# Expert rows of a mixture-of-experts layer in 24 blocks of two 64-row halves, each half with an expert of its own, instead of 31 blocks of 128 rows with one

## The reference

```python
logits = jnp.einsum('th,eh->te', x, gate_w)              # 1024 tokens, 16 experts
topk_w, topk_idx = jax.lax.top_k(softmax(logits), 2)
combine = jnp.sum(one_hot(topk_idx, 16) * topk_w[..., None], axis=1)
gu = jnp.einsum('th,ehj->etj', x, w_gate_up)             # 256 -> 2 x 176
h = silu(gu[..., :176]) * gu[..., 176:]
y = jnp.einsum('eti,eih,te->th', h, w_down, combine)     # 176 -> 256
y = y + swiglu(x @ shared_gate_up, 352) @ shared_down
```

## Time and profile before

| | us |
|---|---|
| runs | 254.44, 252.72, 254.32 |
| median | 254.32 |
| the profiled execution | 252.71 |
| its span (first to last instruction) | 250.7 |

### The profile page before, as it was taken

One profiled execution on the slowest core, in us unless ns is written; L12 is line 12 of the kernel. 1 busy time (PEld: TensorE's weight loads), 2 busy tenths in 40 slices (PEclk: granted clock), 3 DMA queues, 4 the chain that ended last, 5 costly groups with the idle time before them and its releaser, 6 DMA issues.

```text
span 250.7 us, 5232 instructions
## 1 busy us (share of the span) xinstructions
PE 237.4 (95%) x1660; PEld 177.2 (71%) x1660; DVE 148.5 (59%) x452; ACT 129.3 (52%) x465; POOL 92.5 (37%) x110
## 2 busy tenths in 40 slices
PE   8969799999999999999999999799999999999995
PEld 6635475666766677898788787567777777777784
DVE  1568888887889856437896588653223232323184
ACT  2146988989889898540524216124343434343440
POOL 2111211112111100102662004655777777777460
PEclk9999999999999999999999999999999999999999
DMA  7999877100005400006013000222333333343495
GB/s 217 267 366 387 283 174 171 53 3 3 3 0 160 171 3 3 1 3 229 1 41 129 0 3 4 63 68 81 105 105 107 105 95 112 89 102 111 144 338 188
DMA packets 20388, 28.10 MB, mean 112 GB/s; under 512 B 2369, under 2 KB 17355, under 8 KB 20363
## 3 DMA queue, kind: packets, MB, share of 16 engines
q1 hardware_dynamic: 16683, 19.01, 24.5%
q0 software_dynamic: 2976, 8.13, 11.0%
q10 hardware_dynamic: 704, 0.64, 0.8%
HBM read 21.61 MB, written 6.16 MB: 111 GB/s over the span
## 4 chain that ended last, share of the span: by engine, by line
PE 71%; ACT 13%; DVE 8%; issue 4%; DMA 1%; POOL 1%; ACTq 0%; POOLq 0%; DVEq 0%
PE bank L898 15%; PE bank L910 11%; ACT pr_s L1010 10%; PE bank L829 8%; PE bank L531 5%; PE bank L573 4%; PE bank L560 3%; PE bank L879 3%; PE bank L889 3%; PE bank L658 2%; PE bank L536 2%; PE bank L623 2%; PE bank L649 1%; PE bank L668 1%; DMA qx_s<-ffn_in,prT 1%
## 5 line engine op out<-in xcount | busy, mean ns | idle before, releaser
L1010 ACT ACTIVATE pr_s<-bank,mx 128x128 f32<-128x128 f32 x128 | 45.2, 383 | 8.0 <-DVE mx L1236 8.0
L898 PE MATMUL bank<-gu_s,bxT 128*128 x124 | 41.7, 460 | 0.2 <-DVE bxT L1561 0.2
L1567 DVE TENSOR_TENSOR pr_s<-bank,pr_s 128x176 f32<-128x176 f32 x31 | 10.6, 341 | 51.6 <-ACT pr_s L1165 50.9
L492 POOL DMA_INDIRECT expert_out<-by,prT x31 | 31.0, 1000 | 14.8 <-ACT by L1000 7.5
L487 POOL DMA_INDIRECT qx_s<-ffn_in,prT x31 | 30.1, 972 | 14.6 <-issue 8.2
L1000 ACT ACTIVATE prT<-bank 128x512 f32<-128x512 f32 (+1 forms) x63 | 31.1, 497 | 2.9 <-PE bank L573 1.8
L910 PE MATMUL bank<-dn_s,prT 88*128 x124 | 31.7, 379 | 0.0
L1010 ACT ACTIVATION_READ_ACCUMULATOR pr_s<-bank,mx 128x1 f32 x128 | 28.6, 224 | 0.0
L898 PEld LDWEIGHTS bank<-gu_s,bxT 128*128 128x128 f32 x124 | 21.2, 190 | 7.2 <-issue 0.4
L1000 ACT ACTIVATE by<-bank 128x256 f32<-128x256 f32 x31 | 11.9, 383 | 23.5 <-PE bank L910 21.9
L1236 DVE TENSOR_REDUCE mx<-bank 128x4 f32<-128x512 f32 x32 | 20.5, 683 | 4.7 <-PE bank L560 4.7
(11 more groups left out here) (194 smaller groups left out, 438.2 us busy)
## 6 DMA issues: line engine op xcount, KB each, us to landing
gu_s<-in_w_gu SPq DMA_DIRECT2D x8, 704.0 KB, 7.0
dn_s<-in_w_dn SPq DMA_DIRECT2D x4, 704.0 KB
gu_s<-in_ctx_in SPq DMA_DIRECT2D x2, 512.0 KB, 9.2
ffn_in<-x_s SPq DMA_DIRECT2D x4, 256.0 KB, 2.4
cv_s<-expert_out SPq DMA_DIRECT2D x4, 256.0 KB, 4.1
x_s<-expert_out SPq DMA_DIRECT2D x4, 256.0 KB, 5.7
out<-x_s SPq DMA_DIRECT2D x7, 128.0 KB, 3.6
gu_s<-in_x_t SPq DMA_DIRECT2D x1, 768.0 KB, 10.7
```

Of the source, the lines that this page charges most:

```text
L492: pool.indirect_dma_start(expert_out[:], bass.IndirectOffsetOnAxis(ap=idx[:, 1, k:k + 1], axis=0), by[:, k % RB, :], None).then_inc(dma_sc ...
L898: last = mm(bank[2 + i % 2][:, 0:2 * I], bxT[:, i % 2, k, :], gu_s[:, k, bass.ds(e, 1), :], start=k == 0, stop=k == KD - 1)
L1010: last = nc.scalar.activation(pr_s[:, n % 2, h, :], score_bank(n)[:, h * T:(h + 1) * T], ACT.Exp, bias=mx[:, n % 4, h:h + 1], accum_out=de ...
```

## The change

A block now has two halves of 64 rows with an expert each. Expert e's first 64 rows are always the *upper* half (partitions 64 to 127) of block e, for e = 0 to 15. What an expert has beyond 64 rows goes in halves of 64 into the lower halves of blocks 0 to 15 and then into both halves of blocks 16 to 23. So there are at most `MORE` = 32 of these further halves and `BLOCKS` = 24 blocks. The lower half's expert is read from a register as before; the upper half's is fixed for blocks 0 to 15, and for blocks 16 to 23 its weights are loaded once more from memory by SP into four staged buffers (`gu_x`, `dn_x`), each with semaphores of its own for up and down weights. The staged buffers take the memory of the first stages' weights and buffers, which are therefore put into one tensor, `early`. The arrays of the expert weights are laid out on the host so that the 128 rows of both k lie together.

PE: each of the up and down matmuls becomes two with 64 stationary columns. `slot_table` gets 64 matmuls instead of 32. Ahead of the loop, `shared_up(3, 0)` moves ahead of `block_transpose(0)`, with the register loads between its matmuls, and `expert_up(0)` ahead of `block_transpose(1)`. DVE's arithmetic of places gets more and wider operations, and DVE takes half of `num_b` from POOL.

```diff
+HT = T // 2
+MORE = 2 * ((SLOTS - 1) // HT // 2 + 1)
-BLOCKS = (SLOTS + E * (T - 1)) // T
+BLOCKS = E + (MORE - E) // 2
+HALVES = 2 * BLOCKS
+THRESHOLDS = B * T // HT - 1
+SB = 4
...
+def more_of(i):
+    return i if i < E else E + 2 * (i - E)
...
+        staged = early[0][:, 0:SB * (KD * 2 * I + 2 * D)].rearrange("p (r n) -> p r n", r=SB)
+        gu_x = staged[:, :, 0:KD * 2 * I].rearrange("p r (k n) -> p r k n", k=KD)
+        dn_x = staged[0:IH, :, KD * 2 * I:].rearrange("p r (k n) -> p r k n", k=2)
...
             def expert_weights(k, e):
                 sp.dma_start(gu_s[:, k, e:e + 4, :],
-                             w_gu[e:e + 4, k * 128:(k + 1) * 128, :].rearrange("e p n -> p e n")).then_inc(ld_gate_up, 16)
+                             w_gu[e:e + 4, :, k, :].rearrange("e p n -> p e n")).then_inc(ld_gate_up, 16)
...
+            sp.wait_ge(dve_block_experts, 1)
+            staged_expert = [sp.value_load(bei[0:1, more_of(E + j) + 1:more_of(E + j) + 2], min_val=0, max_val=E - 1)
+                             for j in range(BLOCKS - E)]
+            sp.wait_ge(pe_expert_up, RB)
+            for j in range(BLOCKS - E):
+                e = staged_expert[j]
+                if j >= SB:
+                    sp.wait_ge(pe_expert_up, E + j - SB + 1)
+                sp.dma_start(gu_x[:, j % SB], w_gu[bass.ds(e, 1), :, :, :].rearrange("e p k n -> p (e k) n")).then_inc(dma_staged_up[j % SB], 16)
+                if j >= SB:
+                    sp.wait_ge(pe_expert_down, E + j - SB + 1)
+                sp.dma_start(dn_x[:, j % SB], w_dn[bass.ds(e, 1), :, :, :].rearrange("e p k n -> p (e k) n")).then_inc(dma_staged_down[j % SB], 16)
             sp.wait_ge(dve_ring, 1)
...
             pool.wait_ge(dve_block_hot, 1)
-            for k in range(2):
-                last = nc.gpsimd.tensor_tensor(num_b[:, 0, k * B:(k + 1) * B, :], num[:, k * B:(k + 1) * B, :],
-                                               tabr[:, R_TOK:R_TOK + B].unsqueeze(2).to_broadcast([128, B, BLOCKS]), ALU.mult)
-            last.then_inc(pool_block_numbers, 1)
+            nc.gpsimd.tensor_tensor(num_b[:, 0, 0:B, :], num[:, 0:B, :],
+                                    tabr[:, R_TOK:R_TOK + B].unsqueeze(2).to_broadcast([128, B, HALVES]), ALU.mult).then_inc(pool_block_numbers, 1)
...
-            def shared_up(q, c, halves=(0, 1)):
+            def shared_up(q, c, halves=(0, 1), between=()):
...
+                        for i in between[KD * j + k:KD * j + k + 1]:
+                            read_expert(i)
...
-                pe.wait_ge(dve_slot_hot, 1)
+                pe.wait_ge(dve_slot_hot, 2)
...
-                            last = mm(bank[4][:, k * BLOCKS:(k + 1) * BLOCKS], hot[:, k * B + t, :],
-                                      num_b[:, f, k * B + t, :], start=t == 0 and f == 0, stop=t == B - 1 and f == 1)
+                            for u in range(2):
+                                last = mm(bank[4][u * HT:(u + 1) * HT, k * BLOCKS:(k + 1) * BLOCKS], hot[:, k * B + t, :],
+                                          num_b[:, f, k * B + t, u * BLOCKS:(u + 1) * BLOCKS],
+                                          start=t == 0 and f == 0, stop=t == B - 1 and f == 1, skip_group_check=True)
...
+                if i >= E:
+                    pe.wait_ge(dma_staged_up[(i - E) % SB], 16 * ((i - E) // SB + 1))
                 for k in range(KD):
-                    last = mm(bank[2 + i % 2][:, 0:2 * I], bxT[:, i % 2, k, :], gu_s[:, k, bass.ds(e, 1), :],
-                              start=k == 0, stop=k == KD - 1)
+                    mm(bank[2 + i % 2][0:HT, 0:2 * I], bxT[:, i % 2, k, 0:HT], gu_s[:, k, bass.ds(e, 1), :],
+                       start=k == 0, stop=k == KD - 1, skip_group_check=True)
+                    last = mm(bank[2 + i % 2][HT:T, 0:2 * I], bxT[:, i % 2, k, HT:T],
+                              gu_s[:, k, i, :] if i < E else gu_x[:, (i - E) % SB, k, :],
+                              start=k == 0, stop=k == KD - 1, skip_group_check=True)
                 last.then_inc(pe_expert_up, 1)
...
+                if i >= E:
+                    pe.wait_ge(dma_staged_down[(i - E) % SB], 16 * ((i - E) // SB + 1))
                 for k in range(2):
-                    last = mm(bank[4 + i % 2][:, 0:D], bhT[:, i % 2, k, :], dn_s[:, k, bass.ds(e, 1), :],
-                              start=k == 0, stop=k == 1)
+                    mm(bank[4 + i % 2][0:HT, 0:D], bhT[:, i % 2, k, 0:HT], dn_s[:, k, bass.ds(e, 1), :],
+                       start=k == 0, stop=k == 1, skip_group_check=True)
+                    last = mm(bank[4 + i % 2][HT:T, 0:D], bhT[:, i % 2, k, HT:T],
+                              dn_s[:, k, i, :] if i < E else dn_x[:, (i - E) % SB, k, :],
+                              start=k == 0, stop=k == 1, skip_group_check=True)
...
             shared_down(2)
+            pe.wait_ge(dve_block_experts, 1)
+            shared_up(PAIRS - 1, 0, between=range(RB - 1))
             block_transpose(0)
-            pe.wait_ge(dve_block_experts, 1)
-            for i in range(RB - 1):
-                read_expert(i)
             pe.wait_ge(ld_gate_up, 16 * 8)
             pe.wait_ge(ld_down, 16 * 4)
-            shared_up(PAIRS - 1, 0)
+            expert_up(0)
             block_transpose(1)
-            expert_up(0)
...
-            link(V.tensor_scalar_mul(nb[:, 2, :], nb[:, 1, :], float(T)))
+            link(V.scalar_tensor_tensor(nb[:, 2, :], nb[:, 1, :], float(HT), tabr[:, R_BASE:R_BASE + E], ALU.mult, ALU.add))
             shared_mul(1, 2)
-            link(V.tensor_tensor(t128[:, 0], bank[2][:, 0:B * E].rearrange("p (t e) -> p t e", e=E),
-                                 nb[:, 2, :].unsqueeze(1).to_broadcast([128, B, E]), ALU.add))
+            rank = bank[2][:, 0:B * E].rearrange("p (t e) -> p t e", e=E)
+            link(V.scalar_tensor_tensor(t128[:, 0], rank, float(HT), nb[:, 2, :].unsqueeze(1).to_broadcast([128, B, E]),
+                                        ALU.is_ge, ALU.mult))
+            link(V.tensor_tensor(t128[:, 1], rank, t128[:, 0], ALU.add))
...
+            link(V.scalar_tensor_tensor(posf[:, 0, :], s8[:, 2:4, :].rearrange("p k t -> p (k t)"), float(HT), posf[:, 0, :],
+                                        ALU.mult, ALU.add))
...
+            dve.wait_ge(dve_block_hot, 1)
+            V.tensor_tensor(num_b[:, 0, B:2 * B, :], num[:, B:2 * B, :],
+                            tabr[:, R_TOK:R_TOK + B].unsqueeze(2).to_broadcast([128, B, HALVES]), ALU.mult).then_inc(dve_slot_hot, 1)
```

More of the change, by code:

```diff
@@ L55 @@
 C_N = C_IOTA + E
-R_THR, R_LOW, R_BLK, R_SLOT, R_TOK, R_DUMMY = (int(v) for v in np.cumsum([0, B, E * E, BLOCKS, T, 2 * B]))
-R_RING = R_DUMMY + BLOCKS
-R_N = R_RING + RB
+R_THR, R_LOW, R_BLK, R_SLOT, R_TOK, R_DUMMY = (int(v) for v in np.cumsum([0, THRESHOLDS, E * E, HALVES, HT, 2 * B]))
+R_RING, R_MORE, R_BASE, R_N = (int(v) for v in R_DUMMY + np.cumsum([BLOCKS, 2 * RB, MORE, E]))
+def more_of(i):
+    return i if i < E else E + 2 * (i - E)
 def constants():
@@ L85, in routing_constants @@
     p = np.arange(128)[:, None]
-    c[:, R_THR:R_THR + B] = 128.0 * np.arange(B)
+    c[:, R_THR:R_THR + THRESHOLDS] = HT * (1.0 + np.arange(THRESHOLDS))
     c[:, R_LOW:R_LOW + E * E] = (np.arange(E)[None, :] < np.arange(E)[:, None]).reshape(1, -1)
-    c[:, R_BLK:R_BLK + BLOCKS] = np.arange(BLOCKS)
-    c[:, R_SLOT:R_SLOT + T] = np.arange(T)
+    lower = [E + more_of(i) for i in range(BLOCKS)]
+    upper = [i if i < E else E + more_of(i) + 1 for i in range(BLOCKS)]
+    c[:, R_BLK:R_BLK + HALVES] = lower + upper
+    c[:, R_SLOT:R_SLOT + HT] = np.arange(HT)
+    c[:, R_MORE:R_MORE + MORE] = np.arange(MORE)
+    c[:, R_BASE:R_BASE + E] = E * HT - HT - HT * np.arange(E)
     c[:, R_TOK:R_TOK + B] = T * np.arange(B)
     c[:, R_TOK + B:R_TOK + 2 * B] = p + 1
-    c[:, R_RING:R_RING + RB] = RB - 1 - np.arange(RB)
+    c[:, R_RING:R_RING + RB] = E + 1 + 2 * (RB - 1 - np.arange(RB))
+    c[:, R_RING + RB:R_RING + 2 * RB] = 2 * E + 2 * (RB - 1 - np.arange(RB))
     c[:, R_DUMMY:R_DUMMY + BLOCKS] = DUMMY + T * np.arange(BLOCKS) + p + 1
@@ L131, in decoder_layer, with first_half @@
         halfpow = sb("halfpow", [128, B])
-        wq_s = sb("wq_s", [128, QW])
-        wkv_s = sb("wkv_s", [KPH, 2, NOPE + D])
-        wout_s = sb("wout_s", [128, KD, D])
+        early = [sb("early", [128, QW + 2 * (NOPE + D) + 3 * KD * D + XH * HD + 4 * KD * D + 2 * (QP + KP) + 2 * T + 4 * T])[:], 0]
+        def first_half(*shape):
+            flat, at = early
+            early[1] = at + math.prod(shape)
+            part = flat[:, at:early[1]]
+            if len(shape) == 2:
+                return part.rearrange("p (a b) -> p a b", a=shape[0])
+            if len(shape) == 3:
+                return part.rearrange("p (a b c) -> p a b c", a=shape[0], b=shape[1])
+            return part
+        wq_s = first_half(QW)
+        wkv_s = first_half(2, NOPE + D)[0:KPH]
+        wout_s = first_half(KD, D)
         lnq_s = tab[:, C_LN:C_LN + 2]
```

(29 more changed lines are left out.)

36 lines of the change are left out of this document (18 added, 18 removed).

## The result

| | before | after |
|---|---|---|
| median, us | 254.16 | 258.11 |
| runs, us | 252.72 to 254.44 (4) | 257.18 to 259.28 (4) |
| ratio to before | 1 | 1.0169, interval 1.0112 to 1.0227 |
| profiled execution, us | 252.71 | 257.18 |
| its span, us | 250.7 | 255.4 |

The changed kernel is 1.7% slower, 3.95 us by the medians and 4.7 us by the spans. The forecast was 258.0, and +4.4 on the span.

What follows compares the result with a forecast made beforehand. PE, busy 95% of the span, bounds the kernel, its moving columns setting the pace. Loop +0.9, prologue +2.1, stalls +2.2 and tail -0.8 make +4.4 us on a span of 250.7; forecast 258, range 250 to 262.

Steps and rivals of the forecast that it cites:

- Streaming side by side: Up and down matmuls: two 64-column halves run abreast at full rate, so a block's streaming stays 2.49 us.
- The switches: Block loop: two tiled and two full-width stretches a turn cost 2 x (0.14 + 0.15) = 0.58 us; turn 3.07.
- Four turns, not seven: Block loop: the read-back path counts only to the last used block, down in turn 23 instead of 27: -9.96 us.
- The stalls: Staged weight loads on SP come 1.1 us too late at blocks 21 and 23: +2.2 us, from 0 to +4.
- The prologue: Ahead of the loop: router arithmetic, longer slot_table and new order put expert_up(3) at 171.8: +2.1 us, from +1.0 to +3.
- The end: Read-back path: fewer dummy scatters beside the reads, -0.5 us, and its slack of 0.3 goes, -0.3; tail -0.8.
- Loop: Block loop: four turns fewer -9.96, 20 longer turns +11.6, turn 22 -0.5, turn 23 -0.2; sum +0.9 us.
- cheap switches: Rival, block loop: 64-column tiles switch without the 0.58 us, turn falls to POOL's 2.57; -4.6 us, 249.5; chance 0.2.
- halves one after another: Rival, up and down matmuls: halves not side by side, 2.05 us more a block; +47 us, 300; chance 0.03.
- PE as the end: Rival, end: 12.8 us of PE work follow the last down; 6.7 us below the sum, 252; chance 0.04.
- no stalls: Rival: staged loads take 3.0 us and half the prologue goes; +1.1 us, 255; chance 0.22.
- The slow clock at the end: Rival, end: PE idles some 4 us, its last four records take 1.7 instead of 0.87 us; +0.9, 259; chance 0.1.

Runs made afterwards that it cites:

- b_halves: Kernel before, still 31 blocks, with each up and down matmul split into two of 64 stationary columns: 269.37 us, ratio 1.065 to before.
- a_order: Changed kernel with block_transpose(i + 2) ahead of expert_up(i) in the loop: 253.35 us, ratio 1.000 to the kernel before, turns of 2.77 us.
- b_28: Kernel before with BLOCKS = 28, leaving out three blocks that hold only dummies: 253.21 us, ratio 0.999 to before.
- a_queue: Changed kernel with SP's four later up loads queued ahead of the four later down loads: 255.83 us, ratio 1.011 to the kernel before.
- a_busy: Changed kernel with 22 dummy matmuls ahead of PE's wait for the hidden product of shared_mul(3, 1): 258.14 us, ratio 1.021 to the kernel before.

## Why the prediction was right

**Streaming side by side: right.** The row was of tiles with 32 columns; two tiles of 64 run side by side as well, and the block's streaming stayed at 2.49 us.

**The switches: right, 0.58 a turn.** 3.07 was forecast, and all six kernels of the table with four stretches a turn have it. Both terms, 0.14 for a tiled and 0.15 for a full-width stretch, came out within 0.02 us in *b_halves*, and *a_order* took away half of them. The drain on a change of tiling mode that the Trainium skill names (TensorEngine Tiling (Array Packing), Key Properties) is borne out: instructions of the same count cost 0.30 us less a turn where the mode changes twice a turn instead of four times.

**Four turns, not seven: right.** The reads of `expert_out` start on block 20's scatter (235.86, landed 238.27), after turn 23, and *b_28* shows that dummy blocks behind the last used one cost nothing in time. Seven blocks fewer were 17.4 us of PE's work, of which the path to the end saw 10.

**The stalls: right in place and cause**, at blocks 21 and 23; 0.8 and 1.0 us instead of 1.1 each. The loads took 3.3 and 3.0 us and not 3.8, which alone would have made it 0.6 and 0.3. Two things that the term left out gave most of it back: 0.24 us from a load's landing to the first matmul (225.95 to 226.18), and turn 22, which is shorter by its missing block transpose and so covers 0.5 us less of the second load. *a_queue* gave 2.0 back where the term was 2.2.

**The prologue: too dear.** +2.1 us was the term, +0.5 was measured (170.18 against 169.67, both by the chain). Two sizes were wrong. `slot_table` with 64 matmuls took 1.12 us (154.31 to 155.43) where I had 0.025 us for each and 0.2 for switches, 1.8: pairs in the two column tiles overlap there too, which I had granted to the fp32 matmuls and not to these. And it started at 154.31, not 154.7. POOL's product of 384 elements took 1.68 us and was done at 153.84, where I had scaled 2.4 from two of 248; what `slot_table` then waited for was DVE's own half, done at 154.26, and not POOL as the term had it:

```profile
152.16 1.68 POOL L522 TENSOR_TENSOR qx_s<-qx_s,wm_s 128x384 bf16<-128x384 f32 x1 [16.99 <-DVE qx_s L1585]
...
153.07 1.19 DVE L1590 TENSOR_TENSOR qx_s<-qx_s,wm_s 128x384 bf16<-128x384 f32 x1
```

So `slot_table` ended at 155.43, 0.3 us later than before and not 1.4. That is 1.1 of the 1.6; the other 0.5 is in the steps after it, 0.25 up to `expert_up(2)` (12.76 us from the end of `slot_table`, where I had 13.0) and 0.2 from there to `expert_up(3)` (1.99 for 2.2). The 3.08 us that I had scaled from are two products of the same size, of 2.52 and 0.60 us: the first ran beside DVE's 2.28 us for `hot` (150.96 to 153.24), the second, at 153.70, came after it. So the time went by what ran beside it and not by the number of elements, and scaling by elements was the wrong step; an experiment that sets the two apart was not made.

**The end: too cheap.** This is the one term with the wrong sign. It was -0.8: -0.5 for fewer scatters beside the reads and -0.3 of slack. From the reads to the end it was +1.3 (17.1 against 15.8), 2.1 more than forecast, in three parts.

- The lower clock, some 0.95 us (*a_busy*). It had been named as a rival with 0.9 us, rightly sized, but it wasn't in the sum, and no row of before showed it. The idle stretch was 5.4 us and not 4, and eight records were slow; at 0.43 us each the first four are through at 250.4, just before the last product is done (250.52), so four count.
- The reads. The fewer scatters brought nothing to be seen: the last wait of the weighing for a read ends at 247.0, 8.7 us after the first read's issue, and before at 243.0, 8.2 after; the last product comes 0.5 us later after the first read instead of 0.5 earlier. Why was not tried, and the same stretch differs by 1.1 us between profiles (*a_busy*).
- The slack. From the last product to the last addition were 1.34 us before, where 1.21 to 1.23 at full clock is all that the step needs, so only some 0.1 us was to spare and not 0.3.

**The sum.** Loop +0.9, prologue +0.5 and stalls +1.8 make +3.2; the reads start 3.5 us later. By the starts in the timeline (`expert_up(3)` at 170.11 against 169.51, `expert_down` of the last used block at 234.12 against 230.67) the prologue is +0.6 and the loop without its waits +1.0. The forecast had the reads 5.2 us later (at 240) and then 0.8 less; measured are 3.5 and then 1.3 more, +4.7 for +4.4. So the turn, the count of turns and the stalls carry the forecast, and that the total is this close is luck: the prologue was 1.6 too high and the stalls 0.4, the end 2.1 too low.

The rivals: cheap switches fell with the turn of 3.07; halves one after another with starts 0.01 us apart; PE as the end with its wait of 5.4 us; no stalls with the two loads in the chain. The slow clock at the end came true, within the forecast's range.

## What to carry to other kernels

A reordering of an array into tiles is priced by how often an instruction stream changes shape: here some 0.14 us for each stretch, so stretches of one shape are put together before blocks are made smaller. Work left out counts only on the path that sets the end: find the last item that something waits for, count the turns to *it*, and look at what becomes late next, here a load behind another load's wait in a queue and a product behind the weighing in DVE's order.

## What the runs showed of the hardware

- Column tiles of 64 run side by side at the full rate of each, fp32 with 128 and 88 rows (eight records of 352 columns in 1.33 us for 1.19 of four), and a change between tiled and full width costs 0.13 to 0.15 us for each stretch, the same as with 32 columns.
- While PE stood idle for over 5 us at the end, the granted clock fell from 1.00 to 0.50, and the step from the last product to the last addition took 2.17 us instead of 1.21. Dummy matmuls in that stretch kept it at 1.00. The Trainium skill (TensorE: Matmul & The Clock Gate, Part 1: The HAM clock gate) holds that idling lowers the clock; the traces agree.
- The same drop of the clock 20 us into some executions, for 3.4 to 10 us, moves all behind it by 1.8 to 5 us. It isn't of the change: *b_28*, the kernel before with three dummies fewer, shows it in its profile. What brings it on was not tried; PE's idle stretches there (from 14 us on) are 0.9 us at most, not over 5 as at the end.
